# A GNN layer on one Trainium2 core: who finishes the last four row tiles, and in which order their stores leave

## What is computed

```python
h = jnp.maximum(_layernorm(x, axis=-1), 0.0)
deg = jnp.sum(adj, axis=1, keepdims=True) + 1e-05
adj_norm = adj / deg
h_neigh = adj_norm @ h
out = h_neigh @ W_neigh.T + b_neigh + h @ W_self.T + b_self
return x + jax.nn.relu(out)
```

## Time and profile before

| | |
|---|---|
| median of 3 runs | 419.63 us (419.06 to 420.13) |
| the profiled execution | 419.79 us, of which the span from the first to the last instruction is 418.0 us |
| TensorE busy | 410.0 us, 98% of the span, granted clock 0.996 of full speed |
| VectorE, ScalarE, GpSimd busy | 373.5, 207.5, 131.2 us |
| DMA | 83.99 MB, mean 201 GB/s |

### The profile page before, as it was taken

The page is one execution under the profiler, slowest core; times in us unless marked ns, Lnnn a source line. Parts: engine busy times, 40 slices in busy tenths (PEclk is TensorE's granted clock), DMA queues, the critical chain, the costliest instruction groups (busy, mean ns, idle before and its releaser), DMA issues.

```text
span 418.0 us, 5575 instructions
## 1 busy us (share of the span) xinstructions
PE 410.0 (98%) x2005; PEld 344.6 (82%) x2005; DVE 373.5 (89%) x461; ACT 207.5 (50%) x266; POOL 131.2 (31%) x107
## 2 busy tenths in 40 slices
PE   7999999999999999999999999999999999999995
PEld 4788888888888888888888988888888888888884
DVE  4899989999999979999599999989797996979944
ACT  3787667745435534553356445345353644526411
POOL 4667477410025912042207214305200302003021
PEclk9999999999999999999999999999999999999998
DMA  8988999899887176546343755535645454454001
GB/s 268 407 285 315 335 289 318 258 247 284 261 274 166 44 283 225 196 153 218 134 150 107 266 181 200 189 121 178 222 151 201 152 201 159 151 194 169 34 0 52
DMA packets 25339, 83.99 MB, mean 201 GB/s; under 512 B 2784, under 2 KB 4320, under 8 KB 25312
## 3 DMA queue, kind: packets, MB, share of 16 engines
q1 hardware_dynamic: 22864, 75.77, 51.2%
q0 software_dynamic: 2016, 7.34, 8.8%
q10 hardware_dynamic: 432, 0.52, 0.4%
HBM read 79.43 MB, written 4.19 MB: 200 GB/s over the span
## 4 chain that ended last, share of the span: by engine, by line
PE 95%; DVE 2%; issue 1%; POOL 1%; DMA 1%; DVEq 0%; POOLq 0%
PE banks L628 76%; PE banks L687 10%; PE banks L678 2%; PE banks L644 2%; PE banks L645 2%; PE banks L646 2%; DMA x_sb<-x_in 1%; DVE adj_lo L437 1%; POOL rstd L273 1%; PE banks L729 0%; PE banks L660 0%; PE banks L661 0%; PE banks L662 0%; DVE own L589 0%; DVE stats L406 0%
## 5 line engine op out<-in xcount | busy, mean ns | idle before, releaser
L304 ACT ACTIVATE adj_hi<-adj_raw 128x1024 fp32r<-128x1024 f32 x127 | 134.0, 1057 | 129.7 <-PE banks L628 127.6
L437 DVE TENSOR_TENSOR adj_lo<-adj_raw,adj_hi 128x1024 fp32r<-128x1024 f32 x127 | 165.4, 1305 | 13.4 <-ACT adj_hi L304 12.9
L449 DVE TENSOR_TENSOR total<-total,adj_raw 128x1024 f32<-128x1024 f32 x106 | 132.8, 1253 | 0.0
L628 PE MATMUL banks<-adj_hi,h_hi 128*128 128x512 f32 x472 | 128.2, 393 | 0.9 <-ACT adj_hi L304 0.9
L628 PE MATMUL banks<-adj_hi,h_lo 128*128 128x512 f32 x472 | 126.4, 389 | 0.3 <-DVE h_lo L429 0.3
L628 PE MATMUL banks<-adj_lo,h_hi 128*128 128x512 f32 x472 | 126.2, 389 | 0.0
L628 PEld LDWEIGHTS banks<-adj_hi,h_lo 128*128 128x128 f32 x472 | 88.5, 188 | 19.4 <-DVE h_lo L429 0.7
L628 PEld LDWEIGHTS banks<-adj_lo,h_hi 128*128 128x128 f32 x472 | 88.6, 188 | 18.5
L628 PEld LDWEIGHTS banks<-adj_hi,h_hi 128*128 128x128 f32 x472 | 86.5, 188 | 18.7 <-ACT adj_hi L304 2.1
L264 POOL TENSOR_TENSOR x_sb<-x_sb,own 128x1024 f32<-128x1024 f32 x7 | 49.2, 7030 | 121.4 <-ACT own L366 121.4
L258 POOL TENSOR_TENSOR own<-own,b_sum 128x1024 f32<-128x1024 f32 x8 | 23.3, 2909 | 80.4 <-ACT own L351 80.4
(11 more groups left out here) (78 smaller groups left out, 337.4 us busy)
## 6 DMA issues: line engine op xcount, KB each, us to landing
adj_raw<-adj_in SPq DMA_DIRECT2D x128, 512.0 KB, 4.2
total_dma<-adj_in POOLq DMA_DIRECT2D x14, 512.0 KB, 8.0
x_sb<-x_in SPq DMA_DIRECT2D x14, 256.0 KB, 7.3
rows_out<-x_sb SPq DMA_DIRECT2D x7, 512.0 KB, 2.9
rows_out<-x_sb SPq DMA_DIRECT2D x3, 128.0 KB, 1.8
x_sb<-x_in ACTq DMA_DIRECT2D x1, 256.0 KB, 6.8
own<-w_neigh SPq DMA_DIRECT2D x1, 256.0 KB, 5.7
own<-w_self SPq DMA_DIRECT2D x1, 256.0 KB, 5.6
```

The lines of the kernel that those rows point to most:

```text
L304: nc.scalar.activation(adj_hi[:, s % RING, :, :], adj_raw[:, s % RAW, :, :], ACT.Copy).then_inc(s_hi, 1)
L437: nc.vector.tensor_tensor(adj_lo[:, r, :, :], adj_raw[:, s % RAW, :, :], adj_hi[:, r, :, :].bitcast(F32), ALU.subtract).then_inc(s_lo, 1)
L449: nc.vector.tensor_tensor(total[:, q % 2, :, :], total[:, q % 2, :, :], adj_raw[:, s % RAW, :, :], ALU.add).then_inc(s_add, 1)
L628: done = nc.tensor.matmul(banks[:, MAIN[q % 2][k], :], m[:, j, k * P:(k + 1) * P], part[:, r, a, :], start=(j == 0 and stage == 0), stop=F ...
```

## The change

Tile 1 of the last block goes from ScalarE and GpSimd to VectorE: the loop of the one-instruction relu and x add runs over t = 1, 2, 3. ScalarE keeps the relu and GpSimd the x add of tile 0 alone. SyncE issues its three stores in the order 0, 1, 3. Tile 2's store stays on ScalarE's queue.

```diff
-            for b in (3, 0, 1):
+            for b in (0, 1, 3):
                 row = slice((Q - 1) * UI + b, (Q - 1) * UI + b + 1)
                 sp.wait_ge(s_tail[b], 1)
                 sp.dma_start(out[:, row, :], x_sb[:, row, :]).then_inc(s_out, 16)
...
             add_bias(Q - 1)
-            for t in range(2):
-                row = (Q - 1) * UI + t
-                pool.wait_ge(s_relu, Q + t)
-                nc.gpsimd.tensor_tensor(x_sb[:, row, :], x_sb[:, row, :], own[:, t, :], ALU.add).then_inc(s_tail[t], 1)
+            row = (Q - 1) * UI
+            pool.wait_ge(s_relu, Q)
+            nc.gpsimd.tensor_tensor(x_sb[:, row, :], x_sb[:, row, :], own[:, 0, :], ALU.add).then_inc(s_tail[0], 1)
...
-            for t in range(2):
-                act.wait_ge(s_last, t + 1)
-                nc.scalar.activation(own[:, t, :], own[:, t, :], ACT.Relu).then_inc(s_relu, 1)
+            act.wait_ge(s_last, 1)
+            nc.scalar.activation(own[:, 0, :], own[:, 0, :], ACT.Relu).then_inc(s_relu, 1)
             act.wait_ge(s_tail[2], 1)
...
-            for t in range(2, UI):
+            for t in range(1, UI):
                 row = (Q - 1) * UI + t
                 dve.wait_ge(s_last, t + 1)
```

## The result

| | before | changed |
|---|---|---|
| median of 20 runs each | 419.72 us | 418.91 us |
| range | 419.06 to 420.39 | 417.88 to 419.87 |
| ratio, with its 95% interval | | 0.9981 (0.9973 to 0.9988) |
| span of the profiled execution | 418.0 us | 417.2 us |

The gain is 0.80 us, between 0.5 and 1.1. It is real, and smaller than the 0.3% that was taken as the limit of what can be told.

The account below looks back on a forecast made before the run. The prediction took the kernel's end to be bound by three issues in one queue, all begun after the last tile. A gain of 1.00 us from a median of 419.63 gave 418.63 us, range 418.1 to 419.3.

Parts of the forecast that it names:

- The bound: End of last block: three store issues in SyncE's queue, all begun after the last tile; tile 0 ready for 1.57 us.
- GpSimd holds VectorE up: VectorE's last-block relu and add: 0.53 us of waiting for GpSimd gone, 0.37 added, tile 3 ready 0.17 earlier.
- Rival 2: VectorE's tail: the 0.94 isn't GpSimd's doing, last issue as late as now; 419.6 us, no change; chance 0.05.
- The last issue: SyncE's queue at the end: last store issue moves from 415.75 to 414.72, 1.03 us earlier.
- The transfers: DMA bursts of the last stores: work of three bursts sets the end at 416.25, a gain of 1.00 us.
- Rival 3: Last store finds DMA engines free, or short lead and lossless overlap: gain 1.22, 418.41 us; chance 0.17.
- What follows the last byte: After the traffic: SyncE's wait for the landing and closing barrier, 0.75 us, stays unchanged.
- Rival 1: ScalarE's and SyncE's store issues get in each other's way: gain 0.85 us, 418.78 us; chance 0.10.
- Rival 4: GpSimd's x add of tile 0 loses its turn, stores queue behind it: 0.55 us later, 420.18 us; chance 0.05.

Follow-up runs that it names:

- e1: Kernel before with only SyncE's store order changed from 3, 0, 1 to 0, 1, 3; ratio 0.9982, median 418.84 us against 419.55.
- e5: Kernel before without GpSimd's x add of tile 1, whose store waits for ScalarE's relu instead; one execution, 418.06 us beside 418.49 of before.
- e3: Changed kernel with tile 2's store at the end replaced by an earlier store of a finished block 6 tile; ratio 0.9972, median 418.54 us.
- e2: Changed kernel with SyncE's old store order 3, 0, 1 put back; ratio 0.9994, median 419.61 us.
- e8: Changed kernel profiled once more with nothing changed, to see how well the tail repeats; one execution, 418.56 us beside 418.49 of before.
- e4: Changed kernel with tile 0's store moved to ScalarE's queue: ScalarE issues 0 and 2, SyncE 1 and 3; ratio 0.9979, median 418.64 us.
- e6: Changed kernel with GpSimd's x add of tile 0 also waiting for VectorE's fourth join; one execution, 419.15 us beside 418.49 of before.
- e9: Changed kernel with an extra two-SBUF-input VectorE instruction ahead of the three L592, GpSimd's add waiting for it; one execution, 419.52 us beside 420.77 of before.
- e7: Changed kernel with GpSimd's x add of tile 0 also waiting until VectorE finished tile 1; one execution, 419.74 us beside 418.49 of before.
- e10: Changed kernel with a PSUM-reading VectorE instruction between first and second L592, GpSimd's add waiting for it; one execution, 420.03 us beside 420.77 of before.

## Why the prediction was right, point by point

- **The bound.** "Three issues in one queue, all begun after the last tile": shown by e1, in which only their order is changed. The order alone brings 0.75 of 0.85.
- **GpSimd holds VectorE up.** Forecast: tile 3 ready 0.17 earlier, with a duration of 0.41 per tile. Measured: 0.41 twice, and tile 3 at 2.69 instead of 2.89, 0.20 earlier; e5 shows the cause. Rival 2 (no faster VectorE) is out.
- **The last issue.** Forecast 1.03 earlier, measured 1.05.
- **The transfers.** Forecast: 1.00 earlier. Measured: 0.85, and this is the term that was off. The end was forecast at 416.25, or 4.27 from the first join, and is at 4.37. That 0.10 is made of small pieces. 0.03 was my rounding of the bound of 416.28 to 416.25. Tile 1's burst began at about 415.07, or 3.04 from the first join, where 3.02 was used (0.02). The four bursts are 1.59 us of work, 0.40 each where 0.39 was counted, for the last three 0.02. The remaining 0.03 is below the step in which the end is read. The other 0.05 is the start of the difference: 417.25, the edge of a stretch, was taken for the end of the traffic before, which was 417.20. Rival 3 (the last store finds the engines free, 1.22) needed the other bursts out of the way; with one of them gone, in e3, the gain is 1.15, so the count of work was the right way to price this term in the changed kernel.
- **What follows the last byte.** 0.75 was held fixed. By the table above it is 0.80 before, in the changed kernel and in e2, and 0.75 in all the others, the second profile of the changed kernel (e8) among them. It doesn't depend on the order, within these steps.
- **Rival 1** (the two queues' issues hinder each other). ScalarE's issue of 414.42 begins within SyncE's from 414.19 to 414.61, and they take 0.35 and 0.42, as long as without each other. In e4 four issues follow one another on two queues at 0.34 and 0.35. The largest effect in these tails is 0.03: in e6 ScalarE's issue from 414.36 overlaps SyncE's of 414.08 and 414.47 and takes 0.38, and in e9 the same. So the lock wait that the Trainium skill's Perfetto Trace Analysis describes under "DMA Instruction — HWDGE (DVE, Sync)", a part of an issue's recorded length, isn't seen in the changed kernel, and is at most 0.03 in the other tails. The prediction had priced a wait of 0.23.
- **Rival 4** (GpSimd loses its turn). It did not happen, because GpSimd starts 0.56 ahead, as the prediction argued. Its mechanism is real: e7 shows it, at 0.36 of traffic and 0.31 of span against the 0.55 that was priced. But the point from which it decides was wrong: a start after the first L592 is not enough, as e6 shows. The Trainium skill's SBUF — State Buffer, "Who interferes with whom", has the one that issues first hold the ports for that instruction; in e7 and e10 GpSimd, waiting since tile 2's instruction, is passed over by tile 3's as well, so the rule alone doesn't account for them. One reading behind this rival was too simple: block 0's row was not all instructions with two inputs in SBUF, as the prediction had it. A copy with one input stands in it, and the row keeps its pace through it while GpSimd's add, from 132.52 to 147.89, goes on waiting:

```profile
141.47 0.68 DVE L446 COPY total<-adj_raw 128x1024 f32<-128x1024 f32 x1
```

The chances: within 0.3% was given 0.69, and the ratio is 0.9981. The change lies inside the limit chosen, and 20 runs of each kernel still resolve it as a gain.

## What to carry to other kernels

Where several engines finish parts of the last result, issue the stores in the order in which the parts are ready: a store that waits for the last part, put first in an in-order queue, turns the others' early readiness into time after the end. Once that is right, count the DMA work of the last stores; four of 128 KB are 1.6 us here, and when they run as one block, a faster last part buys little: the last issue 0.29 earlier than in e1 brought 0.10 of traffic. And before giving GpSimd a share of a tail to relieve VectorE, look at whether it reads SBUF beside VectorE instructions with two inputs there: here the second x add cost VectorE 0.53 us, more than the 0.37 of doing that tile itself.

## What the runs showed of the hardware that was not expected

- A change of 0.8 us in 420 was priced to 0.2 us from one trace, while single executions scatter by more than 1 us (the first join begins between 410.74 and 412.03 in the profiles). Counted from the first join, the two profiled executions of the changed kernel agree within 0.03 us up to the end of the traffic.
- Whether GpSimd gets in between two such instructions of VectorE or is kept out to the end of the row changed with no difference in the recorded moment of more than 0.01 us. In one case the x add took 0.77, in the other 1.10, and VectorE's next instruction 0.95 or 0.42.
